# Graph attention kernel: key products in eight tiles of the tensor array instead of two, without block-diagonal keys

## The reference

```
vcq   = [x, q_exp]                      # q_exp = cond of the batch, 0 where a row of x sums to 0
self  = vcq @ W_self.T + b_self
for d in (0, 1):
    A     = adj (d=0) or its transpose (d=1), first 20 columns      # [N, 20, 11] of 0/1
    qh, kh = heads of self @ Wq[d].T + bq[d],  heads of self[:, :20] @ Wk[d].T + bk[d]
    aff   = qh . kh / sqrt(32)                                      # [N, 16 heads, 20 keys]
    aff   = where(A.sum(-1) > 0, aff, -9e15) + A @ w_bias + b_bias
    w     = softmax(aff)
    out  += per head (w @ self[:, :20]) @ Wout[d] + bout[d]
y = x + relu(self + out)
```

## Time and profile before

| what | us |
|---|---|
| median of 3 runs (595.75 to 599.45) | 596.0 |
| the profiled execution, its own time | 594.92 |
| its span in the trace | 592.9 |

### The profile page before, as it was taken

The page is one execution under the profiler, slowest core; times in us unless marked ns, Lnnn a source line. Parts: engine busy times, 40 slices in busy tenths (PEclk is TensorE's granted clock), DMA queues, the critical chain, the costliest instruction groups (busy, mean ns, idle before and its releaser), DMA issues.

```text
span 592.9 us, 11310 instructions
## 1 busy us (share of the span) xinstructions
PE 582.7 (98%) x4303; PEld 497.2 (84%) x4303; DVE 452.6 (76%) x654; ACT 412.2 (70%) x830; POOL 439.5 (74%) x400
## 2 busy tenths in 40 slices
PE   9999999999999999999999999999999999999994
PEld 6977798888989898888888898989888888888882
DVE  4896877788777787868687886868786868768676
ACT  4748656786868597777778776768866767866542
POOL 0311199966898986699997599898668989867963
PEclk9999999999999999999999999999999999999999
DMA  8985334275674848295756838386846747583335
GB/s 309 431 311 147 100 107 157 77 213 151 182 210 144 224 120 246 69 259 149 232 159 175 213 106 249 103 243 139 231 128 207 180 161 224 155 221 59 74 107 185
DMA packets 42869, 106.06 MB, mean 179 GB/s; under 512 B 12479, under 2 KB 26303, under 8 KB 36415
## 3 DMA queue, kind: packets, MB, share of 16 engines
q1 hardware_dynamic: 40654, 89.61, 47.3%
q0 software_dynamic: 2160, 15.73, 13.7%
HBM read 85.84 MB, written 19.47 MB: 178 GB/s over the span
## 4 chain that ended last, share of the span: by engine, by line
PE 92%; DVE 3%; POOL 3%; DMA 1%; issue 0%; ACT 0%; DVEq 0%; SPq 0%
PE aff L582 36%; PE gen L513 10%; PE gen L515 10%; PE gen L514 10%; PE aff L549 8%; PE tp L596 4%; PE gen L643 3%; PE gen L653 2%; PE gen L596 1%; PE tp L513 1%; POOL z L1277 1%; PE tp L514 1%; PE tp L515 1%; DVE wol L1105 1%; DMA qT<-in_qT 1%; PE gen L429 1%
## 5 line engine op out<-in xcount | busy, mean ns | idle before, releaser
L1277 POOL TENSOR_TENSOR z<-z,mx 128x640 f32<-128x640 f32 x63 | 87.2, 1385 | 43.8 <-DVE mx L1036 43.8
L582 PE MATMUL aff<-gh,sfh 128*128 128x320 f32 x504 | 117.7, 315 | 0.1
L582 PE MATMUL aff<-gh,sfl 128*128 128x320 f32 x504 | 114.8, 309 | 0.0
L582 PE MATMUL aff<-gl,sfh 128*128 128x320 f32 x504 | 114.8, 309 | 0.0
L1265 POOL TENSOR_TENSOR z<-cb,bx 128x640 f32<-128x640 f32 x64 | 102.1, 1689 | 11.1 <-PE tp L515 10.2
L884 ACT ACTIVATE z<-z 128x640 f32<-128x640 f32 x63 | 46.6, 739 | 84.6 <-POOL z L1277 83.9
L513 PE MATMUL gen<-xh,w1h 128*128 128x512 f32 x256 | 104.1, 407 | 0.1
L515 PE MATMUL gen<-xh,w1l 128*128 128x512 f32 x256 | 101.2, 395 | 0.0
L514 PE MATMUL gen<-xl,w1h 128*128 128x512 f32 x256 | 101.2, 395 | 0.0
L1262 POOL TENSOR_TENSOR sfl<-sff,sfh 128x512 fp32r<-128x512 f32 x48 | 64.5, 1473 | 43.1 <-ACT sfh L749 43.1
L582 PEld LDWEIGHTS aff<-gh,sfh 128*128 128x128 f32 x504 | 83.2, 188 | 13.0 <-issue 12.9
(11 more groups left out here) (164 smaller groups left out, 1122.1 us busy)
## 6 DMA issues: line engine op xcount, KB each, us to landing
x<-in_x SPq DMA_DIRECT2D x16, 1024.0 KB, 7.0
xn<-in_xn SPq DMA_DIRECT2D x31, 512.0 KB, 6.6
sff<-in_x POOLq DMA_DIRECT2D x15, 1024.0 KB, 9.2
out_y<-sff SPq DMA_DIRECT2D x15, 1024.0 KB, 4.2
msk<-in_mask SPq DMA_DIRECT2D x16, 880.0 KB, 7.9
cb<-c_scratch SPq DMA_DIRECT2D x16, 320.0 KB, 4.8
nz<-nz_scratch SPq DMA_DIRECT2D x16, 256.0 KB, 3.7
wkT<-in_wkT SPq DMA_DIRECT2D x4, 512.0 KB, 8.2
```

The lines of the kernel that those rows point to most:

```text
L582: mm = nc.tensor.matmul(aff[:, t % 2, half, 0:SH], s, g[:, b - starts[group(b)], f, half * SH:(half + 1) * SH], start=(f == 0 and i == 0), ...
L1277: nc.gpsimd.tensor_tensor(zt(slot, t), zt(slot, t), heads(mx, t, M), ALU.subtract).then_inc(s_sub, 1)
```

## The change

Key products are made with the keys as they are loaded (`khc`), on tiles of 32 rows (one head) and 64 columns (half a chunk of features): four heads by two halves are eight tiles. A block is one chunk f for all four groups of heads, 64 matmuls with 60 moving columns (40 in a group of two batches). Each head h has a bank of its own, aff[:, h // 2, h % 2], so a block fills four banks. PE waits for both units of the block before. `bd`, its clearing and `k_blocks` are gone, and the units of eviction keep their size. KEYS becomes (3, 3, 3, 2). In all batches the last label copies and the edge terms come ahead of the exponential of tile 3. In batches with key products DVE sums the labels of direction 0 ahead of the total of tile 3 and those of direction 1 behind the second add_query, and `g_low` of unit 6 comes behind the last add_query; ACT puts the last sf_high ahead of evict_wt 2 and a row sum behind it. In the prologue a block each stands ahead of self_feat 2, values(2, 0), self_feat 3 and values(2, 1). SP waits for the products of a group in place of `k_blocks`.

```diff
-        bd = sb("bd", [P, GD, GB, 2, M])
...
-        KEYS = (3, 3, 3, 1)
+        KEYS = (3, 3, 3, 2)
 
         def g_part(g, pair, u, r):
 
             f, k = u // G2, u % G2
-            return g[:, 0:sizes[pair], f].rearrange("p b (g r e) -> p r b g e", g=HG, r=2)[:, r, :, 2 * k:2 * k + 2]
+            return g[:, 0:sizes[pair], f].rearrange("p b (g h e) -> p h b g e", g=HG, h=H4)[:, 2 * k + r]
...
-                    sp.wait_ge(s_bd, group(b) + 1)
+                    sp.wait_ge(s_g, group(b) * FC + FC)
                     load_k(group(b) + 1)
...
                     if between is not None and c == KEYS[f]:
-                        for k in range(G2):
-                            key_products(between, G2 * f + k)
-
-            def key_products(pair, u, first=False):
-                f, k = u // G2, u % G2
-                if u == 0:
-                    pe.wait_ge(s_bd, pair + 1)
-                if u < 2 and not first:
-
-                    pe.wait_ge(s_z, starts[pair] * T - 1 + u)
-                if u >= 2:
-                    pe.wait_ge(s_gl, pair * GU + (u - 1))
-
-                for hg in (2 * k, 2 * k + 1):
+                        key_products(between, f)
+
+            def key_products(pair, f, first=False):
+                if f == 0:
+                    pe.wait_ge(s_khin, pair * 16 + 16)
+                    if not first:
+
+                        pe.wait_ge(s_z, starts[pair] * T)
+                else:
+                    pe.wait_ge(s_gl, pair * GU + f * G2)
+
+                for hg in range(HG):
                     for d in range(D):
-                        for r in range(2):
-                            rows = slice(r * P // 2, (r + 1) * P // 2)
-                            bank = aff[:, k, r, 0:sizes[pair] * SH // 2].rearrange("p (b g h d m) -> p g d b h m", b=sizes[pair], g=2, h=2, d=D)
-                            mm = nc.tensor.matmul(bank[:, hg % 2, d], wq[rows, hg, d, f * P:(f + 1) * P], bd[rows, hg * D + d, 0:sizes[pair]],
-                                                  start=True, stop=True)
+                        for c in range(2):
+                            cols = slice(f * P + c * P // 2, f * P + (c + 1) * P // 2)
+                            for h in range(H4):
+                                rows = slice(h * DH, (h + 1) * DH)
+                                bank = aff[c * P // 2:(c + 1) * P // 2, h // 2, h % 2, 0:sizes[pair] * SH // 2].rearrange("p (b g d m) -> p g d b m", g=HG, d=D, m=M)
+                                mm = nc.tensor.matmul(bank[:, hg, d], wq[rows, hg, d, cols], khc[rows, 0:sizes[pair], hg * D + d, :], start=True, stop=True)
                 mm.then_inc(s_g, 1)
...
-            def k_blocks(pair):
...
             def evict_g(pair, u):
-                act.wait_ge(s_g, pair * GU + (u + 1))
+                act.wait_ge(s_g, pair * FC + u // G2 + 1)
...
-                if next_g:
-                    k_blocks(pair)
-                elif ahead >= 1 and b > 0:
+                if ahead >= 1 and b > 0:
                     next_labels(n, 0)
...
                 exponential(b, slot, 1)
                 if ahead >= 1 and b > 0:
-                    next_labels(n, 0 if next_g else 1)
+                    next_labels(n, 1)
                 exponential(b, slot, 2)
                 if ahead == 2:
                     row_sums(b + 2, 0, b * 32 + 48)
                 if ahead >= 1 and b > 0:
-                    next_labels(n, 1 if next_g else 2)
+                    next_labels(n, 2)
+                    edge_terms(n)
...
                     evict_g(pair, 0)
                     evict_g(pair, 1)
                     sf_high(n, other, 0)
-                    if b > 0:
-                        next_labels(n, 2)
-                        edge_terms(n)
                     sf_high(n, other, 1)
...
-            nc.vector.memset(bd[:], 0.0).then_inc(s_zero, 1)
...
                 total(b, slot, 2)
                 add_query(n, other, 0)
+                if next_g:
+                    dve.wait_ge(s_bx, b * T + T)
+                    label_sum(n, 0)
                 total(b, slot, 3)
                 if next_g:
                     g_low(pair, 0)
                     g_low(pair, 1)
                 add_query(n, other, 1)
                 if next_g:
+                    label_sum(n, 1)
                     g_low(pair, 2)
                     g_low(pair, 3)
                 add_query(n, other, 2)
...
                 if next_g:
                     g_low(pair, 4)
                     g_low(pair, 5)
-                    g_low(pair, 6)
...
                 add_query(n, other, FC - 1)
                 if next_g:
+                    g_low(pair, 6)
                     g_low(pair, 7)
```

More of the change, by code:

```diff
@@ L157, in build @@
         s_wo, s_wq, s_id, s_idr = sem("wo_in"), sem("wq_in"), sem("ident_in"), sem("ident_rounded")
-        s_zero, s_w1h, s_w1l, s_kvh, s_kvl = sem("zeroed"), sem("w1_high"), sem("w1_low"), sem("kvx_high"), sem("kvx_low")
+        s_w1h, s_w1l, s_kvh, s_kvl = sem("w1_high"), sem("w1_low"), sem("kvx_high"), sem("kvx_low")
         s_wkh, s_wkl, s_woh, s_wol = sem("wk_high"), sem("wk_low"), sem("wo_high"), sem("wo_low")
@@ L178, in build @@
         s_sfd = sem("sf_low_part")
-        s_bd = sem("k_blocks_done")
         s_g, s_gh, s_gl = sem("g_ready"), sem("g_high_done"), sem("g_low_done")
@@ L207, in build @@
         XP = 2
-        KEYS = (3, 3, 3, 1)
+        KEYS = (3, 3, 3, 2)
         def g_part(g, pair, u, r):
             f, k = u // G2, u % G2
-            return g[:, 0:sizes[pair], f].rearrange("p b (g r e) -> p r b g e", g=HG, r=2)[:, r, :, 2 * k:2 * k + 2]
+            return g[:, 0:sizes[pair], f].rearrange("p b (g h e) -> p h b g e", g=HG, h=H4)[:, 2 * k + r]
         def g_bank(pair, u, r):
-            return aff[:, u % G2, r, 0:sizes[pair] * SH // 2].rearrange("p (b g e) -> p b g e", b=sizes[pair], g=2)
+            return aff[:, u % G2, r, 0:sizes[pair] * SH // 2].rearrange("p (b g e) -> p b g e", b=sizes[pair], g=HG)
         def key_bank(g):
@@ L670, in _ @@
             key_products(0, 0, True)
+            self_feat(0, 2)
             key_products(0, 1, True)
-            self_feat(0, 2)
+            values(2, 0)
             key_products(0, 2, True)
+            self_feat(0, 3)
             key_products(0, 3, True)
-            values(2, 0)
-            key_products(0, 4, True)
-            key_products(0, 5, True)
-            self_feat(0, 3)
-            key_products(0, 6, True)
-            key_products(0, 7, True)
             values(2, 1)
@@ L749, in sf_high @@
                 nc.scalar.activation(sfh[:, f, :], sff[n % 3][:, f, :], ACT.Copy).then_inc(s_sfh, 1)
-            def k_blocks(pair):
-                act.wait_ge(s_khin, pair * 16 + 16)
-                for h in range(H4):
-                    r = slice(h * DH, (h + 1) * DH)
-                    last = nc.scalar.activation(bd[r, :, 0:sizes[pair], h % 2, :], khc[r, 0:sizes[pair]].rearrange("p b g m -> p g b m"), ACT.Copy)
-                last.then_inc(s_bd, 1)
             def evict_g(pair, u):
-                act.wait_ge(s_g, pair * GU + (u + 1))
+                act.wait_ge(s_g, pair * FC + u // G2 + 1)
                 for r in range(2):
@@ L849, in _ @@
             labels(0, range(0, L, LG))
-            act.wait_ge(s_zero, 1)
-            k_blocks(0)
             labels(0, range(1, L, LG))
@@ L939, in batch @@
                 evict_wt(b, 1)
-                if ahead == 2:
-                    row_sums(b + 2, 1, b * 32 + 64)
                 if next_g:
@@ L944, in batch @@
                     evict_g(pair, GU - 1)
-                evict_wt(b, 2)
-                sf_high(n, other, FC - 1)
+                    sf_high(n, other, FC - 1)
+                    evict_wt(b, 2)
+                    if ahead == 2:
+                        row_sums(b + 2, 1, b * 32 + 64)
+                else:
+                    if ahead == 2:
+                        row_sums(b + 2, 1, b * 32 + 64)
+                    evict_wt(b, 2)
+                    sf_high(n, other, FC - 1)
                 evict_wt(b, 3)
```

3 lines of the change are left out of this document (removed).

## The result

| what | before | after |
|---|---|---|
| median of 4 runs (lowest to highest), us | 596.67 (595.75 to 599.45) | 619.03 (614.63 to 623.72) |
| the profiled execution and its span | 594.92, 592.9 | 623.72, 621.6 |

The ratio is 1.037, with a 95% interval of 1.033 to 1.041: slower by 22 us, where 597.0 was forecast and 611 was the end of the range. The profiled execution is the longest of the four; its span is 28.7 us above that of before, so a sum over its trace has to reach 28.7, not 22.

A forecast was written before the change was run, and what follows sets the result against it. PE was taken as the bound. Group batches +4.2, last group -1.2 and prologue -2.0 summed to +1.0 us on 594.9, giving 595.9; with the execution 1.1 below the median, 597.0. The range was 588 to 611 us.

The forecast's parts named there:

- What bounds the kernel, where the price of a block lies: PE bounds the kernel; a key-product block costs 2.18 us, set by weight loads of 128 columns, not by moving columns.
- The block itself, 0.98 us: Key products on eight tiles: 0.98 us inside for 1.79, block 1.35 for 2.18, saving 0.83 in each of 24 blocks.
- rival B: Key-product blocks: instruction issue doesn't hold the 7 ns pace; at 15 ns a record +17, 614 us; chance 0.20.
- hides behind the load: Inside a block: the 60 moving columns take 50 ns and are covered by the 64-column load's 58 ns.
- over 1.3 inside: Sign of being wrong: a block taking over 1.3 us inside would point to rival B.
- 1.9 us for each 0.1: Each 0.1 us more in a block costs 0.3 in a group batch and about 1.9 us in all.
- The coarser wait and the moved labels: Batches 1, 4, 7, 10: stalls 2.2, 0.7, 0.4, 0.9 against 3.3 saved, 1.0 us later each; batch 13: -1.2.
- the walk of one batch: Step-by-step timing of batch 1 on PE, ACT and DVE, ending 1.0 us later; applied to batches 1, 4, 7, 10.
- The prologue, -2.0: Prologue: 4 x 0.83 saved, only block 3 waits, 0.9 to 1.3 (upper end taken): -2.0 us.
- Ordinary batches at nothing: Ten batches without key products: tile 3's exponential ends 1.1 us later, but 0.5 of cover remains, so no cost.
- rival D: Ordinary batches: the later exponential uses up the 0.5 us cover, up to 1 us in each of ten: 607; chance 0.11.
- Rival C: Blocks' gain stays because copies run so early that g_low is never last: 577, or 587 with half the stalls; chance 0.17.

The follow-up runs named there:

- experiment 6: Kernel after with four tiles of 32 rows by 128 columns, half as many matmuls and weight loads: 614.96 us, ratio 1.027.
- experiment 5: Kernel after with its eight tiles, but labels, edge terms, label sums, g_low 6 and KEYS ordered as before: 618.21 us, ratio 1.033.
- experiment 9: Kernel after with 32 tiny matmuls (64 instructions with their loads) more at the start: 625.16 us, ratio 1.044.
- experiment 10: Kernel after without DVE's low-part subtractions in groups 2 to 5; blocks and scores wait for ACT's copies instead: 619.57 us, ratio 1.031.
- experiment 11: Kernel before with each key-product matmul split into two of 64 feature columns, four tiles of 64 by 64: 591.30 us, ratio 0.992.
- experiment 12: Kernel before with 64 by 64 tiles and the last block one self-features step later (KEYS 3, 3, 3, 2): 589.60 us, ratio 0.987.
- experiment 1: Kernel before with only the coarse wait: each block waits for both units of the block before: 599.84 us, ratio 1.005.
- experiment 2: Kernel before, its two row tiles kept, with the whole new order of labels, edge terms, sums, g_low 6, last copies and KEYS: 606.50 us, ratio 1.016.
- experiment 3: Kernel before with only label copies and edge terms ahead of tile 3's exponential and label sums at their new places: 605.09 us, ratio 1.011.
- experiment 4: Kernel before with only KEYS 3, 3, 3, 2, g_low 6 behind the last add_query and ACT's new last-copy order: 601.56 us, ratio 1.007.

## Why the prediction was wrong, point by point

*What bounds the kernel, where the price of a block lies:* right. A load of 128 columns holds a tile for 106 ns and more (experiment 6: 1.74 us for 16), and the number of moving columns doesn't matter as long as it is under the load (same experiment, 60 and 40 columns: 1.74 and 1.72 us).

*The block itself, 0.98 us:* mis-sized; it measured 1.36, and 1.29 in groups of two batches, 85 and 81 ns for each round of eight records. Neither the load (58 ns) nor the columns (50 and 33 ns) gives that; 10.6 ns a record, 5.3 an instruction, looks like the rate at which PE is fed. The pace was read from L653, where eight records start 7 ns apart; over the longer series the distance is half as much again. The trace of after has the reason that rival B gave: of block 0 of batch 1 the first 33 records start within 0.29 us, nearly all 7 ns apart, and the other 95 are 11.3 ns apart in the mean, in steps of 8 to 17. The 15 ns at the end of L653's row was the beginning of that. The step that failed is "hides behind the load", which left out a bound of its own for the issue. I had that as rival B, "decides from 1.25 us inside", and as a sign of being wrong (over 1.3 inside). By the prediction's own 1.9 us for each 0.1, the 0.38 is +7 us: 604, inside the range. By the Trainium skill (TensorE: Matmul & The Clock Gate, Back-to-back issue gap) small matmuls don't start closer than about 25 ns; these traces have 10.6 ns over 128 records on different tiles, so it is no bound across tiles.

*The missing term:* the pauses, 17.4 us in the trace of after and 12.5 to 19 in experiments 5, 9 and 10, stand in no term and no rival: the prediction lets a block's records run through once it has begun, and puts the fetch of instructions at nothing without naming it. B said the issue might not hold the pace, and took that to be a slower pace all through. What happens is that the pace holds until the fetched instructions are used up, and PE then stands still until the next 256 are there. This is what carried the result out of the range. Shown are: the place (a fixed count, moved by adding instructions), the need for a dense burst (none with 256 instructions in 7.1 us, and with 128 in 1.1 to 1.7 a single one, a step of 0.50 us, at the 37 such places inside blocks of experiments 6, 11 and 12), and the end (2.2 to 2.5 us after the packet's start). By the Trainium skill (Runtime: NRT & Kernel Launch, Instruction fetch mechanics) an engine fetches its instructions in blocks of 16 KiB, 256 instructions, while it executes those before, and the cost is mostly hidden. The traces agree with the size, and with the cover for the kernel before; for blocks of 256 instructions in 1.4 us they do not. I didn't weigh that section before, and the row that would have called for it was on the profile's page of before: queue 8, 34 packets for 8606 records.

*The coarser wait and the moved labels:* right in mechanism, and close in size. Batch 1: 2.2, 0.7, 0.4 and 0.9 forecast; 1.7, 0.6, 0.45 and 0.95 measured. Batch 1 was to last 39.5 us and lasts 40.3, 0.8 more, which is 4 x 0.36 for the blocks (1.71 in place of 1.35), less the 0.5 by which the waits are shorter and the 0.1 that was rounded up; the last group's first wait was to be 1.6 and is 1.1. Experiments 1 to 4 show each part. What the walk of one batch didn't give is that the next group batches aren't like batch 1: block 1 of batch 7 waited 4.0 us. There ACT's exponential of tile 1 begins 3.4 us before block 0, in batch 4 it is 6.1 us, so ACT and POOL were late against PE; what made them late wasn't followed up.

*The prologue, -2.0:* batch 1's first block came 1.3 us later than before, through one pause of 1.95 us and 1.2 us of slow clock behind it; in experiment 5, with 1.9 us of pauses, it came 0.3 earlier, so without them about 2 us would have been gained. That this is the forecast is luck: four blocks saved 0.50 each and not 0.83, and block 3, which was to wait up to 1.3 us, didn't wait at all.

*Ordinary batches at nothing* (rival D): right, 29.8 us. *Rival C*, the gain stays: no, PE is seen waiting for `gl`. *The clock*, which stood in no step, costs 4.1 us behind long stalls.

*The sum:* the forecast gain of 20 us from blocks was 10.6, the forecast waits of 20 were 16, and pauses and clock came on top with 21.5. (The +4.2 for four batches of +1.0 is 0.2 too much; it changes nothing.)

## What to carry to other kernels

Before splitting matmuls over more tiles, count the instructions that the split issues and the time that they are to take: here 128 in 1.6 us were fed with hardly a stop, and 256 in 1.4 us stopped PE for 0.8 to 2.7 us in 9 of the 24 blocks. Idle time "issue" in the middle of a group of like instructions is the sign, and windows from pause to pause that hold a constant count confirm it. When a block gets shorter, its next limit (loads, moving columns, feed) and the eviction behind it take back most of the gain: price each of them alone, and keep the fine waits; the 64 by 64 tiles took 5 us off alone, and 7 with the later last block.

## What the runs showed of the hardware that was not expected

- TensorE stands still when a burst outruns its instruction fetch: 11 pauses of 0.8 to 2.7 us in after, each at 192 or 193 records (matmul, load and semaphore) above a multiple of 256, each over 2.2 to 2.5 us after the start of a 16 KB packet. It isn't fixed how long after need a packet starts: in experiment 10 one started 1.3 us after PE had stopped. In none of the 14 traces do two packets of the queue start closer together than 3.29 us. What holds one back is open. A wait behind data in the same DMA engines would fit the DMA share of 0.93 before the packets that ended a pause; but bursts and loads fall into the same stretches of a batch, and no run took them apart.
- Over 128 records on eight tiles, matmuls start 10.6 ns apart in the mean (60 columns) and 10.1 (40 columns), with one weight load each.
- On 64 by 64 tiles a pass of 120 fp32 columns takes 101 ns and one of 80 takes 69; on 32 by 128 tiles the load of 128 columns, 109 ns, hides 60 columns in full.
- The clock fell to its lower level behind single stalls of 2.0, 4.4 and 2.7 us (from 334.3 to 337.8, for instance), where the kernel before held the full clock in every such batch. It didn't fall behind a stall of 2.4 us (445.6 to 448.0). In experiment 6 it fell behind two entries of 1.6 us and not behind two others of the same length.
